# A fused vision block: squeeze gate in fewer steps, projection from the lower half first, the sums x + xn on VectorE, and a new written order

## The chip, the cores and the metric

The kernel runs on one core of a Trainium2 chip. Time is the device time of one launch in microseconds (us); three runs gave 5884.94 to 5890.72, median 5888.1. The engines are TensorE (PE, its weight loads PEld), VectorE (DVE), ScalarE (ACT), GpSimd (POOL) and SyncE (SP), which issues all DMAs here. Each works through its own list of instructions in order, and they wait for each other by semaphores.

## The reference

The input is 32 images of 96 channels, 56 x 56. Two layers follow, each a convolution part and a feed-forward part with its own norm and residual. The part that the change touches is layer 0's convolution:

```python
h = einsum('nchw,oc->nohw', x, w_exp)            # 96 -> 576
h = silu(bn(h));  h = silu(bn(depthwise3x3(h)))
s = h.mean(axis=(2, 3))
s = silu(s @ w_se1.T + b_se1)                    # 576 -> 24
s = sigmoid(s @ w_se2.T + b_se2)                 # 24 -> 576
h = einsum('nchw,oc->nohw', h * s, w_proj)       # 576 -> 96
return bn(h) + identity                          # identity is the normed x
```

The image is normed before (xn), and x + xn is what the projection is added to. Behind it come a quantised feed-forward part (96 to 384 to 96, in 8-bit floats), layer 1's convolution (1x1, group norm, gelu, axial shifts by one pixel with 1x1 convolutions and gelus, group norm, 1x1) and a second feed-forward part.

## The kernel before

An image is 96 channels of 3136 positions, cut into eight tiles of seven rows (392 positions); tiles 0 to 3 are the upper half, 4 to 7 the lower. The work is software-pipelined over images: one frame of the program holds layer 0's convolution of image i, and parts of images i+1 (its first norm and expansions), i-1 and i-2. What each engine does in a frame and in which order is written out by hand: the table `TIMES` (lines 52 to 134) gives each step a number per engine, and `timetable` sorts by them. The numbers set the order only. `with_banks` deals three PSUM banks (the ring) to the steps in that order.

The steps that are named here, a step being what one tile or one chunk needs on one engine:
- center_a, var_a, rstd_a, norm_a: the first norm of image i+1. GpSimd's norm_a (line 1110) adds xn to x in the buffer x_in; save_s stores the sum to DRAM, reload_x loads x a second time ahead of it, fetch_s brings the sum back for the projection.
- expand k, dw k h: the 576 channels are five chunks (four and a half). Chunks 0 to 2 are expanded on TensorE and convolved on VectorE, nine taps for each half h of the image (line 965; the first tap, line 962, opens the accumulator). Half 0 of chunk 0 and the rest go through texp and tconv, a convolution on TensorE.
- silu2: ScalarE's activation of the convolved maps, with the channel sums for the gate.
- se1, se2, se3: the gate. TensorE multiplies 21 columns of sums by w_se1 (line 660), ScalarE takes the silu, TensorE multiplies by w_se2 (line 666), VectorE adds the bias (969), ScalarE takes tanh, VectorE makes 0.5 t + 0.5 (972) and scales the projection's weights (977, 979).
- proj: six steps (line 671 and on), three for the upper half and then three for the lower. Each makes one tile whole and a third of the half's fourth tile. x1 (lines 988, 992) adds the projection to x + xn.
- center 0, var 0, rstd 0, norm 0, up, down, add: norm and feed-forward part; the same with 1 and 2 for the later norms.
- conv1, gn, gelu1, shift, combo, fold, sum, conv3, x2: layer 1's convolution. The group norm's chain (lines 1045 to 1077) runs over VectorE, TensorE and GpSimd (the root).

The tap that opens an accumulator of chunk 0 or 1 waits until all six projections of the image before are done, since the projection reads the same buffers.

## Time and profile before

| | before |
|---|---|
| median of 3 runs | 5888.1 us (5884.94 to 5890.72) |
| the profiled execution | 5895.56 us, of which the span of its instructions is 5893.7 us |
| TensorE busy | 5303.1 us, 90% of the span |
| VectorE busy | 4892.0 us, 83% |
| ScalarE busy | 4145.5 us, 70% |
| GpSimd busy | 574.4 us, 10% |
| mean granted TensorE clock | 0.945 of 2.4 GHz |

Busy time is the time in which an engine has at least one instruction under way. Matmuls overlap, so a full TensorE isn't one at its peak. "Idle before" and "waited for" name what released an engine after it had stood still.

### The profile page before, as it was taken

What the parts mean: (1) busy time and instruction counts of PE and PEld (TensorE: products, weight loads), DVE (VectorE), ACT (ScalarE), POOL (GpSimd) and SP (SyncE); (2) the same over time, 40 slices, a digit from 0 to 9 for tenths busy, and PEclk for the clock granted to TensorE, in tenths of its full rate; (3) what the DMA queues carried; (4) which work ended last, traced back from release to release, by engine and by line L of the source; (5) the groups of instructions that cost most, each with busy time, mean ns of one, the idle gap of its engine ahead of it and who ended that gap; (6) DMA issues with size and microseconds to landing.
All of it is one profiled execution on the core that took longest, in us unless ns stands there. A gap on an engine that the chain in (4) does not pass through costs nothing.

```text
span 5893.7 us, 165528 instructions
## 1 busy us (share of the span) xinstructions
PE 5303.1 (90%) x67266; PEld 2773.9 (47%) x67266; DVE 4892.0 (83%) x8119; ACT 4145.5 (70%) x7517; POOL 574.4 (10%) x431
## 2 busy tenths in 40 slices
PE   1889999999999999999999999999999998999986
PEld 0344555444555444555444555444555444555442
DVE  4878988888988888988888988888988888988874
ACT  1467766677867677777767867767867777867766
POOL 1111001111001111001111001111001111001100
PEclk9999999999999999999999999999999999999997
DMA  1334434444433444443444434445443445443433
GB/s 51 84 100 122 105 99 103 116 116 125 105 100 101 115 115 122 105 102 102 117 115 126 102 101 104 118 111 126 102 102 102 116 114 125 104 101 100 113 79 78
DMA packets 467883, 625.04 MB, mean 106 GB/s; under 512 B 81218, under 2 KB 466691, under 8 KB 467035
## 3 DMA queue, kind: packets, MB, share of 16 engines
q1 hardware_dynamic: 467132, 614.44, 41.2%
q8 instruction: 543, 8.90, 0.7%
q14 instruction: 208, 1.70, 0.1%
HBM read 272.13 MB, written 78.68 MB: 60 GB/s over the span
## 4 chain that ended last, share of the span: by engine, by line
PE 51%; issue 24%; DVE 8%; ACT 6%; POOL 6%; DMA 3%; SPq 1%; POOLq 0%; ACTq 0%; DVEq 0%
PE bank L596 21%; PE bank L650 11%; PE b_banks L596 7%; POOL x_in L1110 6%; PE bank L637 4%; PE sums_b L603 3%; PE sums_a L603 2%; DVE conv L965 2%; DMA x_in<-in_x 2%; ACT hidden L879 2%; PE bank L679 1%; ACT hidden L886 1%; DVE bn_stats L1037 1%; PE bank L666 1%; PE bank L660 1%
## 5 line engine op out<-in xcount | busy, mean ns | idle before, releaser
L965 DVE SCALAR_TENSOR_TENSOR conv<-mid,w_dw,conv 128x1568 f32<-128x1568 f32 x1280 | 2339.8, 1843 | 3.6
L761 PE MATMUL b_banks<-shifted,w_combo 128*32 128x392 f32 x6144 | 639.8, 543 | 179.8 <-DMA shifted<-g 115.7
L596 PE MATMUL bank<-xc_a,w_exp 128*32 128x392 f32 x5376 | 714.8, 509 | 43.7 <-DVE xc_a L948 38.7
L1110 POOL TENSOR_TENSOR x_in<-x_in,xc_a 96x392 f32<-96x392 f32 x256 | 509.7, 2000 | 1731.4 <-DVE xc_a L948 1125.4
L679 PE MATMUL bank<-conv,w_proj_gated 128*32 128x392 f32 x1920 | 665.7, 503 | 0.0
L596 PE MATMUL bank<-conv,w_proj_gated 128*32 128x392 f32 x5760 | 652.7, 495 | 0.2 <-DVE w_proj_gated L979 0.2
L596 PE MATMUL bank<-x,centering 128*32 128x392 f32 x4608 | 646.3, 504 | 1.5 <-ACT sq_a L790 0.5
L650 PE MATMUL bank<-phases,w_toeplitz 128*32 128x392 f32 x6144 | 645.1, 494 | 0.8 <-ACT phases L823 0.7
L879 ACT ACTIVATE hidden<-b_banks 128x1176 f16<-128x1176 f32 x512 | 590.6, 1153 | 40.5 <-PE b_banks L596 36.9
L637 PE MATMUL bank<-xc_a,w_exp 128*32 128x448 f32 x4096 | 593.6, 545 | 15.8 <-ACT mid L816 15.4
L886 ACT ACTIVATE hidden<-hidden 128x1176 fp8e5<-128x1176 f16 x512 | 607.3, 1186 | 0.8 <-PE bank L596 0.7
L650 PE MATMUL bank<-phases_on,w_toeplitz 128*32 128x392 f32 x6144 | 598.6, 494 | 2.6 <-DMA phases_on<-phases 2.6
L596 PE MATMUL b_banks<-xn,w_q 128*32 128x392 fp8e5 x6144 | 519.1, 344 | 78.8 <-DVE xn L1014 41.1
L789 ACT ACTIVATE xc<-bank 96x392 f32<-96x392 f32 x256 | 126.3, 493 | 549.6 <-PE sums_a L603 443.5
L834 ACT ACTIVATE conv<-bank,bn_affine 128x392 f32<-128x392 f32 x512 | 347.1, 678 | 192.4 <-PE bank L650 191.6
L988 DVE SCALAR_TENSOR_TENSOR x<-bank,bn_bias,r_a 96x392 f32<-96x392 f32 x192 | 119.4, 622 | 426.9 <-PE bank L679 318.7
L761 PEld LDWEIGHTS b_banks<-shifted,w_combo 128*32 128x32 f32 x6144 | 217.4, 116 | 540.7 <-DMA shifted<-g 276.6
L603 PE MATMUL sums_a<-sq_a,row_select 128*32 128x98 f32 x4096 | 448.5, 256 | 1.5 <-ACT sq_a L790 1.5
L816 ACT ACTIVATE mid<-bank 128x392 f32<-128x392 f32 x672 | 336.5, 501 | 140.1 <-PE bank L596 132.8
L603 PE MATMUL sums_b<-sq_b,row_select 128*32 128x98 f32 x4096 | 421.0, 248 | 1.7 <-ACT sq_b L870 0.8
L1022 DVE TENSOR_SCALAR hidden<-hidden,b_q 128x392 f16<-128x392 f16 x1536 | 397.1, 312 | 18.4 <-ACT hidden L879 17.1
L596 PEld LDWEIGHTS bank<-conv,w_proj_gated 128*32 128x32 f32 x5760 | 230.1, 111 | 379.9 <-issue 370.3
(165 smaller groups left out, 9279.0 us busy)
## 6 DMA issues: line engine op xcount, KB each, us to landing
phases_on<-phases SPq DMA_DIRECT2D x1024, 101.5 KB, 2.4
shifted<-g SPq DMA_DIRECT2D x512, 149.6 KB, 2.7
x_in<-in_x SPq DMA_DIRECT2D x512, 147.0 KB, 2.7
shifted<-g SPq DMA_DIRECT2D x256, 199.5 KB, 3.0
r_a<-rstd_row_a SPq DMA_DIRECT2D x256, 147.0 KB, 3.2
x_plus_norm<-x_in SPq DMA_DIRECT2D x256, 147.0 KB, 2.6
r_b<-rstd_row_c SPq DMA_DIRECT2D x256, 147.0 KB, 2.9
r_b<-rstd_row_b SPq DMA_DIRECT2D x256, 147.0 KB, 2.8
```

The source lines that it names most:

```text
L596: last = mm(o[j:j + QUAD, :], weights[:, j:j + QUAD], x, start=start, stop=stop)
L603: last = mm(VPS[th], ROW[:, VR - 1 - r:VR - 1 - r + QUAD], sq[:, j * VW:(j + 1) * VW], start=(r == 0), stop=(r == VR - 1))
L637: last = mm(ring[bank][32 * q:32 * q + 32, 0:EROWS * WW], WEXP[:, m0:m0 + 32], xc_phase(q, h), start=True, stop=True)
L650: last = mm(ring[bank][32 * p:32 * p + 32, 0:TW], TWZ[:, (3 * g + dx) * 2 + r % 2, :], phase_rows(EB if r < 2 else FB, p, QH, dx), start=( ...
L679: last = mm(ring[bank][C:C + QUAD, 0:TW], weights[:, QUAD * r:QUAD * r + QUAD], tile(maps, NTH - 1, 128), start=start, stop=stop)
L761: last = mm(rows(PB[32 * u:32 * u + 32, m, 0:TW]), WC[:, u // 2, 32 * m:32 * m + 32], SH[t % 2][:, u, :].rearrange("p (h w) -> p h w", w=G ...
L834: f(conv_rows(u, r), rows(ring[bank][:, 0:TW]), ACT.Silu, scale=SCB[:, 0, k:k + 1], bias=SCB[:, 1, k:k + 1], accum_out=SUMS[:, j:j + 1]).t ...
L879: f(Y16[t % 2][:, :, :], PB[:, 0:NHC, 0:TW], ACT.Copy).then_inc(sem["up_evacuated"], 1)
L886: f(Q8[t % 2][:, :, :], Y16[t % 2][:, :, :], ACT.Copy, saturate=False)\
L965: v.scalar_tensor_tensor(out=acc, in0=src, scalar=WDW[:, k, j:j + 1], in1=acc, op0=ALU.mult, op1=ALU.add).then_inc(convolved, 1)
L1022: last = v.tensor_scalar(Y16[t % 2][:, c, :], Y16[t % 2][:, c, :], B1Q[:, g, c:c + 1], 0.0, ALU.add, ALU.max)
L1110: g.tensor_tensor(xl, xl, xc_tile(t), ALU.add).then_inc(sem["xplus_a"], 1)
```

## The change

Five things are changed.

1. The gate. The matmuls over the channel sums are split: 20 of the 21 columns (step se1a) stand ahead, and one, the last half of chunk 2, is left for se1. They write into the bank of the sums of squares, not into the ring. The bias of the second product is a row of its weights (S1 has a constant one below its 24 rows), and this product is made in groups of 32 columns. Tanh reads PSUM, and the 0.5 of 0.5 t + 0.5 is folded into the projection's weights at setup, so that the gated weights are WP t + WP, one VectorE instruction for each of six slices.
2. The projection. The lower half comes first, and a projection waits for each slice of the gated weights by itself, not for all. Everything that follows the order of its tiles (x1, center 0, var 0, the last feed-forward part, store) is turned by four tiles (`turned`).
3. The tap that opens the lower half of chunk 0 or 1 waits for the first three projections of the image before, and the upper half's for all six.
4. The sums x + xn are a VectorE step, xplus_a; GpSimd has none left.
5. `TIMES` has new numbers throughout, so every engine's order is another one.

```diff
     "DVE": {
-        "rstd_a": (5168,), "norm_a": (5622, 5814, 5991, 6773, 6831, 7212, 7671, 7960),
-        "dw 0 1": (8759, 9328, 9453, 9691, 9806, 9869, 9928, 9984, 10404),
+        "xplus_a": (6291, 6995, 7187, 7884, 7974, 8001, 8773, 9160), "rstd_a": (5187,),
+        "dw 0 1": (8468, 8491, 8661, 8691, 8998, 9338, 9348, 9402, 9427),
...
+    def turned(t):
+        return (t + NTH) % NT
...
+            elif name in ("se1a", "se1"):
                 chunk_of = [0] + [k for k in range(1, NDV) for _ in range(2)] + [0] * PH + [NDV] * (2 * PH) + [NCH] * PH
+                late = N_S2 - 1
+                if name == "se1a":
+                    pe.wait_ge(sem["activated2"], at(N_S2 * a + late))
+                    pe.wait_ge(sem["t_activated2"], at(N_TC * (a + 1)))
+                    pe.wait_ge(sem["se_scalar"], at(2 * a - 1))
+                    for j, k in enumerate(chunk_of):
+                        if j != late:
+                            mm(SE1P, SE1[:, k, :], SUMS[:, j:j + 1], start=(j == 0), stop=False)
+                else:
+                    pe.wait_ge(sem["activated2"], at(N_S2 * (a + 1)))
+                    mm(SE1P, SE1[:, chunk_of[late], :], SUMS[:, late:late + 1], start=False, stop=True)
...
                 for k in range(NCK):
-                    last = mm(ring[bank][:, k:k + 1], SE2[:, 128 * k:128 * k + 128], S1, start=True, stop=True)
+                    last = columns(ring[bank][:, k:k + 1], SE2[:, 128 * k:128 * k + 128], S1)
...
                 for k in range(NCH + 1):
-                    weights = WPS[:, k if k < NCH else NCH + h, :]
-                    maps = conv(k, h) if k < NCH else ACC4
+                    if r == 0 and (h == 0 or k == NCH):
+                        pe.wait_ge(sem["se_vector"], at((NCK + 1) * a + (k + 1 if h == 0 else NCK + 1)))
+                    weights = WPS[:, k if k < NCH else NCH + 1 - h, :]
+                    maps = conv(k, 1 - h) if k < NCH else ACC4
...
+            elif name == "se2":
+                act.wait_ge(sem["se_matmul"], at(2 * a + 2))
+                act.wait_ge(sem["se_vector"], at((NCK + 1) * a))
+                f(GATE[:, :], ring[bank][:, 0:NCK], ACT.Tanh, scale=0.5).then_inc(sem["se_scalar"], 1)
...
+            elif name == "xplus_a":
+                t = arg[0]
+                dve.wait_ge(sem["normed_a"], at(NT * n + t + 1))
+                dve.wait_ge(x_loaded[t % XSLOTS], at(16 * (NT // XSLOTS * (2 * n + 1) + t // XSLOTS + 1)))
+                xl = XL[t % XSLOTS][0:C, :]
+                v.tensor_tensor(xl, xl, xc_tile(t), ALU.add).then_inc(sem["xplus_a"], 1)
...
                     if k <= 1:
-                        dve.wait_ge(sem["projected"], at(NPR * m))
+                        dve.wait_ge(sem["projected"], at(NPR * (m - 1) + NTH - 1 if h else NPR * m))
...
-                v.tensor_tensor(WPS[:, 0:NCK, :], WP[:, 0:NCK, :],
-                                GATE[:, 2, :].unsqueeze(2).to_broadcast([128, NCK, C]), ALU.mult)
-                v.tensor_scalar(WPS[CW:128, NCK, :], WP[CW:128, NCK, :], GATE[CW:128, 2, NCH:NCK], None, ALU.mult)\
-                    .then_inc(sem["se_vector"], 1)
+                for k in (*range(NCH), NCK, NCH):
+                    p0, p1, g = (CW, 128, NCH) if k == NCK else (0, CW, k) if k == NCH else (0, 128, k)
+                    v.scalar_tensor_tensor(out=WPS[p0:p1, k, :], in0=WP[p0:p1, k, :], scalar=GATE[p0:p1, g:g + 1],
+                                           in1=WP[p0:p1, k, :], op0=ALU.mult, op1=ALU.add).then_inc(sem["se_vector"], 1)
...
-            elif name == "norm_a":
-                t = arg[0]
-                pool.wait_ge(sem["normed_a"], at(NT * n + t + 1))
```

VectorE, from the gated weights to the middle of the projection, before. L969 to L979 is the gate, L1029 and L1032 an add of the feed-forward part, L988 and L992 are one x1, L1087 is x2, L962 the first tap of the lower half of chunk 0:

```order
L969 TENSOR_TENSOR gate<-bank,b_se 128x5
L972 TENSOR_SCALAR gate<-gate 128x5
L977 TENSOR_TENSOR w_proj_gated<-w_proj,gate 128x480
L979 TENSOR_SCALAR w_proj_gated<-w_proj,gate 64x96
...
L1087 SCALAR_TENSOR_TENSOR x<-b_banks,gn_small,x 96x392
...
L992 SCALAR_TENSOR_TENSOR x<-bank,bn_bias,xc 32x392
L962 TENSOR_SCALAR conv_1<-mid,w_dw 128x1568
L988 SCALAR_TENSOR_TENSOR x<-bank,bn_bias,r_a 96x392
L992 SCALAR_TENSOR_TENSOR x<-bank,bn_bias,xc 32x392
L965 SCALAR_TENSOR_TENSOR conv_1<-mid,w_dw,conv_1 128x1568
```

The same place on VectorE after (L967 is x + xn, L991 a slice of the gated weights, L1000 and L1004 x1, L1100 x2, L980 and L983 taps):

```order
L967 TENSOR_TENSOR x_in<-x_in,xc_a 96x392
L991 SCALAR_TENSOR_TENSOR w_proj_gated<-w_proj,gate 128x96 x4
L991 SCALAR_TENSOR_TENSOR w_proj_gated<-w_proj,gate 64x96 x2
L967 TENSOR_TENSOR x_in<-x_in,xc_a 96x392 x2
...
L1004 SCALAR_TENSOR_TENSOR x<-bank,bn_bias,xc 32x392
L1100 SCALAR_TENSOR_TENSOR x<-b_banks,gn_small,x 96x392
L980 TENSOR_SCALAR conv_1<-mid,w_dw 128x1568
L983 SCALAR_TENSOR_TENSOR conv_1<-mid,w_dw,conv_1 128x1568
L1100 SCALAR_TENSOR_TENSOR x<-b_banks,gn_small,x 96x392
L983 SCALAR_TENSOR_TENSOR conv_1<-mid,w_dw,conv_1 128x1568 x2
L967 TENSOR_TENSOR x_in<-x_in,xc_a 96x392
L1000 SCALAR_TENSOR_TENSOR x<-bank,bn_bias,r_a 96x392
```

Before, the lower half's first tap stood ahead of the last x1 (fifth x1 above it, sixth below) and the others behind it; now it and three more stand between the third and the fourth x1. The sums of x stand ahead of the gated weights and behind them.

TensorE, from the second group norm's last product (L747) to the first projection, before (L660 is se1, L666 se2, b_banks from g conv3, bank from xc_a an expansion, centering a center):

```order
L747 MATMUL sums_b<-gn_small,w_l 96x1
L660 MATMUL bank<-pool_sums,w_se 24x1 x21
L596 MATMUL b_banks<-g,w_scaled 32x392 x6
L666 MATMUL bank<-x 128x1 x5
L596 MATMUL b_banks<-g,w_scaled 32x392 x3
L596 MATMUL bank<-xc_a,w_exp 32x392 x4
L596 MATMUL bank<-x,centering 32x392 x3
L596 MATMUL bank<-conv_0,w_proj_gated 32x392 x3
```

And after (L667 is se1a, L670 se1, bank from x with 32x1 se2):

```order
L667 MATMUL sums_a<-pool_sums,w_se 24x1 x20
L599 MATMUL bank<-xc_a,w_exp 32x392 x4
L758 MATMUL sums_b<-gn_small,w_l 96x1
L670 MATMUL sums_a<-pool_sums,w_se 24x1
L599 MATMUL bank<-xc_a,w_exp 32x392 x4
L599 MATMUL bank<-x 32x1 x20
L599 MATMUL b_banks<-g,w_scaled 32x392 x3
L599 MATMUL bank<-xc_a,w_exp 32x392 x4
L599 MATMUL bank<-conv_1,w_proj_gated 32x392 x3
```

Twenty of the gate's products moved ahead of the group norm's, and two of three conv3 and the center moved behind the start of the projection.

TensorE between the third projection and the fourth, after; before, nothing stood there:

```order
L599 MATMUL bank<-x,centering 32x392 x3
L599 MATMUL b_banks<-g,w_scaled 32x392 x3
L599 MATMUL bank<-x,centering 32x392 x6
L607 MATMUL sums_a<-sq_a,row_select 32x98 x4
L599 MATMUL b_banks<-g,w_scaled 32x392 x3
L599 MATMUL bank<-x,centering 32x392 x3
L599 MATMUL bank<-conv_0,w_proj_gated 32x392 x3
```

Six three-column steps now stand in the middle of the projection.

## Rows read from the trace of the kernel before

**Rows 1.** The page: busy time of each engine, its share of the span, instructions.
```profile
PE 5303.1 (90%) x67266; PEld 2773.9 (47%) x67266; DVE 4892.0 (83%) x8119; ACT 4145.5 (70%) x7517; POOL 574.4 (10%) x431
```
**Rows 2.** Busy time in one frame: engine, busy (instructions); PEclk, DMA share, GB/s.
```profile
2700.00:2874.20 174.20, 162.74 (x2098) 85.35 (x2094) 149.63 (x247) 129.21 (x235) 17.68 (x13) 0.96 0.43 108
```
**Rows 3.** The same in slices: PE, PEld, DVE, ACT, POOL; PEclk, DMA, GB/s.
```profile
2866.00:2876.00 10.00, 8.29 (x99) 4.28 (x102) 6.92 (x16) 2.74 (x9) 2.45 (x3) 0.83 0.58 162
2886.00:2896.00 10.00, 10.00 (x130) 4.35 (x125) 3.76 (x6) 0.00 (x0) 1.02 (x1) 1.00 0.35 96
2916.00:2926.00 10.00, 10.00 (x144) 5.79 (x138) 10.00 (x14) 7.92 (x15) 0.00 (x0) 1.00 0.32 80
```
**Rows 4.** TensorE's waits over the span: for whom; us, times, longest.
```profile
PE b_banks L761 <- DMA shifted<-g: 115.7, 89, 7.1
...
PE sums_b L747 <- DVE gn_small L1070: 55.0, 32, 2.5
...
PE bank L596 <- DVE w_proj_gated L979: 0.2, 1, 0.2
```
**Rows 5.** VectorE's timeline: start, duration, instruction [idle before, releaser].
```profile
2810.39 0.36 DVE L1045 BATCH_NORM_AGGREGATE gn_small<-bn_stats 96x2 f32<-96x48 f32 x1
...
2831.16 0.27 DVE L933 TENSOR_SCALAR r_a<-sums_a 32x98 f32<-32x98 f32 x1 [3.06 <-issue]
...
2861.32 0.37 DVE L1045 BATCH_NORM_AGGREGATE gn_small<-bn_stats 96x2 f32<-96x48 f32 x1
...
2865.52 0.97 DVE L1066 TENSOR_TENSOR gn_small<-gn_small,v_l 96x1 f32<-96x1 f32 x1 [0.44 <-POOL gn_small L1104]
2866.53 0.93 DVE L1068 TENSOR_TENSOR gn_small<-gn_small 96x1 f32<-96x1 f32 x1
...
2873.60 0.15 DVE L969 TENSOR_TENSOR gate<-bank,b_se 128x5 f32<-128x5 f32 x1
...
2896.64 1.04 DVE L962 TENSOR_SCALAR conv<-mid,w_dw 128x1568 f32<-128x1568 f32 x1 [2.00 <-PE bank L679]
```
**Rows 6.** TensorE's timeline, with the same columns (x: instructions merged into the row).
```profile
2794.46 1.17 PE L596 MATMUL b_banks<-g,w_l 128*32 128x392 f32 x9
...
2810.80 0.33 PE L740 MATMUL sums_b<-gn_small,mean_w 96*96 96x1 f32 x2 [0.24 <-DVE gn_small L1045]
...
2821.64 4.15 PE L761 MATMUL b_banks<-shifted,w_combo 128*32 128x392 f32 x24 [1.46 <-DMA shifted<-g]
...
2833.26 2.18 PE L761 MATMUL b_banks<-shifted,w_combo 128*32 128x392 f32 x24
...
2871.97 1.27 PE L666 MATMUL bank<-x 24*128 24x1 f32 x10
...
2875.22 0.52 PE L596 MATMUL bank<-conv,w_proj_gated 128*32 128x392 f32 x2
...
2896.31 1.17 PE L596 MATMUL bank<-x,centering 128*32 128x392 f32 x9
```
**Rows 7.** VectorE's groups by form: count | busy us, mean ns | idle before.
```profile
L965 DVE SCALAR_TENSOR_TENSOR conv<-mid,w_dw,conv 128x1568 f32<-128x1568 f32 x1280 | 2339.8, 1843 | 3.6
...
L948 DVE TENSOR_TENSOR xc_a<-xc_a,r_a 96x392 f32<-96x392 f32 x256 | 154.7, 604 | 23.0 <-DMA r_a<-rstd_row_a 22.8
...
L1070 DVE TENSOR_TENSOR gn_small<-v_l,gn_small 96x1 f32<-96x1 f32 x64 | 9.9, 155 | 2.2
...
L979 DVE TENSOR_SCALAR w_proj_gated<-w_proj,gate 64x96 f32<-64x96 f32 x32 | 8.6, 270 | 0.5
```
**Rows 8.** GpSimd's waits, then its group of sums.
```profile
POOL x_in L1110 <- DMA x_in<-in_x: 606.0, 96, 10.7
...
L1110 POOL TENSOR_TENSOR x_in<-x_in,xc_a 96x392 f32<-96x392 f32 x256 | 509.7, 2000 | 1731.4 <-DVE xc_a L948 1125.4 <-DMA x_in<-in_x 606.0
```
**Rows 9.** ScalarE's timeline: the last silu ahead of the gate, and its Tanh.
```profile
2864.57 1.70 ACT L845 ACTIVATE conv<-conv,bn_affine 128x1568 f32<-128x1568 f32 x1
...
2873.78 0.21 ACT L854 ACTIVATE gate<-gate 128x5 f32<-128x5 f32 x1 [3.02 <-DVE gate L969]
```

132 lines of the change are left out of this document (58 added, 74 removed), and 102 rows, old and new, of the table TIMES.

## Prediction

> **What bounds the kernel now.** I read the page's busy line first, then one frame (one image's turn of the pipeline, 174.2 us here), then ten-microsecond slices of it. TensorE is busy for 5303 of 5894 us, VectorE for 4892 [rows 1]. In the frame TensorE is busy for 162.7 us, VectorE for 149.6 [rows 2], so TensorE idles for 11.5 us and VectorE for 24.6, and the question is where. The slices answer it: in the projection VectorE works 3.76 of 10 us while TensorE is full; just behind it both are full; around the gate TensorE is short, with the granted clock at 0.83 [rows 3]. VectorE can't start the next depthwise taps in the projection: tap 0 of "dw 0 1" is released by the last projection tile at 2896.64 [rows 5]. TensorE's waits lie elsewhere, in the grouped convolution between the two group norms: for the shifted copies 115.7 us in total, for the second norm's affine 55.0. For the gated weights it waited 0.2 us [rows 4].
>
> TensorE's landmarks cut the frame into stages [rows 6]; the projection's start is 2875.22 and its end the 2896.64 of [rows 5]:
> - conv1 (2794.46) to gn 0 (2810.80): 16.3 us, full.
> - gn 0 to gn 1, by VectorE's aggregates 2810.39 and 2861.32 [rows 5]: 50.9 us. TensorE has gaps, VectorE one of 3.06 us, in which rstd_a waits for the sums of squares.
> - aggregate of gn 1 to projection: 13.9 us.
> - projection: 21.4 us.
> - projection's end to the next conv1 (2794.46 + 174.2 = 2968.7): 72.0 us, TensorE full.
> These are 174.5 us for 174.2, since two boundaries are read on another engine.
>
> **The change, part by part.** A three-column step on TensorE (center, conv1, conv3) is two groups of x3; nine instructions took 1.17 us, the last 0.51, so a group costs 0.33 and a step 0.66 [rows 6]. An expansion of four columns has two groups too.
>
> *Gate chain.* Before, from the gate's first VectorE instruction (2873.60) to the first projection matmul it was 1.6 us [rows 5, 6]: an addition, Tanh on ScalarE, an affine, the product over all chunks, and the split chunk's 0.27. Center and expansions covered it, hence the wait of 0.2 us. After, Tanh reads PSUM and VectorE writes six slices of 96 columns; the nearest row is 0.27 us for 64x96 [rows 7], and TensorE may start after the first. Six cost up to 1.6 us of VectorE; the old instructions took the 1.6 us less 0.2 of Tanh [rows 9]: equal. The chain is 1 us shorter and TensorE's second gate step turns from 5 matmuls of 128 columns into 20 of 32; I take that step as unchanged (it took 1.27 us for ten instructions [rows 6]; between half and one and a half times that, so ±0.65). What pays is the order. From the aggregate of gn 1, VectorE has two moved sums and norms, the spread and the last tap of "dw 2 1", about 3.6 us; ScalarE's silu of that half is 1.7 us [rows 9] and its sum is read out behind it, so 5.5; one matmul is left of the first gate step, since the 20 others (1.3 us) went ahead; then two short ScalarE steps [rows 9] around the second gate step, 1.3: 8.2 us to the first slice (5.5 + 0.3 + 0.4 + 1.3 + 0.4 + 0.3), 8.9 when the conv3 and the expansion behind that step are counted. TensorE's own work in the stage falls by 2.0 less 0.7: two conv3 and one center moved behind the start of the projection, an expansion came in. The stage was 13.9; I take 10.4, **-3.5 us**, for what in-order queues will add, with ends 9.4 (-4.5) and 12.9 (-1.0). Two VectorE instructions of the affine took 0.97 and 0.93 us beside GpSimd's sums, where a like one takes 0.155 [rows 5, 7]. That 1.6 us of stretch is part of the gain.
>
> *Projection.* Between proj.0 and proj.5 TensorE now has seven three-column steps instead of two, and two of var: 5 x 0.66 + 0.2 = **+3.5 us**. VectorE gets four more taps, two more x2, one add and one sum there; four taps are 7.4 us at 1.843 [rows 7]. With the others it is some 10 us, and the stage has room: VectorE idled for 6.2 of 10 us in it [rows 3], 13 of the 21.4. Taps on the lower half don't touch the accumulator tiles that the remaining matmuls read. The lower half goes first because the waiting accumulator is the lower one. A late reload of x + xn for x1.3 is now covered by the four taps ahead of it.
>
> *Behind the projection.* Two centers fewer and one expansion of phases fewer up to conv1: -2.1; var pairs -0.1: **-2.2 us**, and the expansion comes back in the next stage, **+0.6**. That 7 us of taps are gone here is worth nothing: TensorE is full [rows 3].
>
> *Group norm 0 to 1.* Taps (17), adds, quants and norms of x are equal in number before and after. One fp8 norm and one sum x + xn are added, 2 x 0.604 = +1.2 [rows 7]; two adds and a norm, 2.2 us of work, moved ahead of rstd_a and fill as much of the gap of 3.06 [rows 5]: -2.2 + 1.2 = **-1.0**. Ends: -1.9, the whole gap filled, and 0, where ScalarE or the shifted copies hold the stage.
>
> *Sums x + xn on VectorE.* Eight of 0.604 are 4.8 us a frame on an engine of 149.6 [rows 2, 7]; GpSimd took 2.0 us each [rows 8]. Of the eight, one is counted above, four lie in the gate stage and three in the projection and behind it. Only what stands ahead of the gate slices counts, and it is in the 8.2 us.
> What the rows show of the shared work is that VectorE's small instructions stretch from 0.155 to 0.97 beside a GpSimd sum [rows 5, 7], while a GpSimd sum stretches to a mean of 2.0 [rows 8]. The Trainium skill ("SBUF — State Buffer", Who interferes with whom) has a rule for that: a VectorE instruction with two SBUF inputs and a GpSimd instruction that reads SBUF exclude each other; the trace agrees.
> VectorE is the second busiest engine, and 1.2 us of new work stand in its fullest stage [rows 1, 2]. The Trainium skill ("Perfetto Trace Analysis", Optimizing Scalar/DVE Operations) would rather move work from a saturated VectorE to GpSimd, but adds that the shared port may void that; by it this change goes the wrong way, which is rival 3.
>
> **The sum.** -3.5 + 3.5 - 2.2 + 0.6 - 1.0 = -2.6 us a frame. With 32 images there are 31 frames from gate to gate: -81 us. Setup gains two short VectorE instructions, under 1 us. The profiled execution took 5895.6 us (span 5893.7); 5895.6 - 81 = 5814.6. The runs' median, 5888.1, is 7.5 lower: **5807 us**. Ends: -4.5 - 1.9 - 2.2 + 0.6 + 3.5 = -4.5 a frame, 5749 us; -1.0 + 0 - 2.2 + 0.6 + 3.5 = +0.9, 5916.
>
> **Rivals.**
> 1. *More comes back.* The first combo took 4.15 us for 24 matmuls that take 2.18 later; ahead of it TensorE had gapped and was at the half clock [rows 6]. If the gaps close, the clock stays up: -2.0 more than the best sum, -6.5 x 31 = -202: 5687 us. For it: both low-clock places lie behind gaps. Against: that combo's gap is a chain (norm, gelu, five copies) that the change hardly touches.
> 2. *Nothing.* VectorE was not what held the combo stage; the copies were (115.7 us) [rows 4], and ScalarE has no less to do. Then group norm 0 to 1 gives 0, the gate stage gives what was moved out of it, 2.0, and its smaller gap 1.6, the projection takes 3.5: -3.6 + 3.5 - 2.2 + 0.6 = -1.7 less what the second gate step costs more, 0.65, and a like amount lost at banks: about -0.4 x 31: 5876 us. For it: TensorE is full in three stages, 16.3 + 21.4 + 72.0 us, and its work is unchanged.
> 3. *The in-order queue pays for GpSimd's waits.* GpSimd waited 606 us for the reload of x, 96 times, 6.3 us each [rows 8], and nobody stood behind it. On VectorE one such sum stands directly ahead of the gate slices and two more ahead of x1.0. The projection's first tile (a sixth of 21.4 - 1.3, 3.3 us) hides two; the one ahead of the slices hides nothing. If the reload lands late there, the gate and the projection start 6.3 us late: -2.6 + 6.3 = +3.7 a frame, 6003 us. It decides from 2.6 us of lateness on. Against: for that sum, tile 3, the reload waits for no store of a slot but only for the centering of all eight tiles, which is done before the combos; tiles 4 and on wait for a store.
> 4. *The stage is VectorE's.* The adds and the order fill it, with its slack in the projection spent, and it ends 1 us later than the middle: -1.0 in the gate stage and +1.2 between the norms: +2.1 a frame: 5953 us.
>
> **How the numbers follow.** Forecast (5749 to 5860) 0.46; rival 1 0.18; rival 2 (5860 to 5900) 0.16; rivals 3 and 4 0.20, of which half lies under 5940. What can be told from no change is 0.2%, 12 us: 5876 to 5900. Faster: 0.46 + 0.18 + 0.07 = 0.71, same 0.11, slower 0.18. The range runs from rival 1 to 5930: 0.08 left out below, 0.1 above.
>
> **What would show it.** Right: the 24 us of VectorE's idleness per frame shrink, with five taps between x1.0 and x1.5; the idle time ahead of rstd_a's first instruction is under 1 us; the aggregate of gn 1 to the first projection matmul is near 10 us; the affine's multiplications take 0.16 us; busy TensorE time is the same. Wrong: VectorE waiting for x_in at its sums; TensorE waiting for w_proj_gated by more than 1 us a frame; TensorE waiting longer for the shifted copies; x1.3 or a center between the projections waiting for a bank. If the gate stage is short and the frame isn't, the loss lies where TensorE was full.

## The result, and the profile after

The changed kernel takes 5681.5 us (median of 4 runs, 5676.0 to 5687.2) where the kernel before took 5889.4 in the same comparison: a ratio of 0.9643, interval 0.9625 to 0.9662. That is 208 us, 3.5%, less. In a second comparison it was 0.9630 (0.9613 to 0.9648). The forecast was 5807 us with a range of 5685 to 5930: the direction was right, the gain was two and a half times the forecast one, and the time lies 3.5 us below the range.

The page of the changed kernel, busy line, answers to [rows 1]:

```profile
PE 5167.6 (91%) x68226; PEld 2777.0 (49%) x68226; DVE 4964.0 (87%) x8441; ACT 4168.4 (73%) x7517; POOL 77.3 (1%) x175
```

TensorE is busy for 135.5 us less, although it has 960 matmul records more. A busy time that shrinks under more work points at the clock: the mean granted clock went from 0.945 to 0.970, up 2.6%, and the busy time fell by 2.6%. VectorE is busy for 72 us more and GpSimd for 497 less.

How long a frame is in the mean, from the first and the last time of the gate's first VectorE instruction. Before, then after (L991 has six instructions a frame, and the row's last start is that of the last one, 1.4 us after its first):

```profile
L969 DVE TENSOR_TENSOR gate<-bank,b_se x32: 148/165/166, 234.8 to 5695.7; 128x5 f32<-128x5 f32 x32
```
```profile
L991 DVE SCALAR_TENSOR_TENSOR w_proj_gated<-w_proj,gate x192: 308/315/321, 234.9 to 5480.9; 128x96 f32<-128x96 f32 x128, 64x96 f32<-64x96 f32 x64
```

(5695.7 - 234.8) / 31 is 176.2 us, and (5480.9 - 1.4 - 234.9) / 31 is 169.2. So a frame lost 7.0 us, and the frame of 174.2 us on which the prediction stood [rows 2] was 2 us shorter than the mean.

The stages of that other, commoner kind of frame before. The columns are those of [rows 2]: stretch, its length, busy time (instructions) of PE, PEld, DVE, ACT, POOL, granted clock, DMA share, GB/s. Second group norm to projection, projection, projection to the next conv1:

```profile
2683.93:2699.51 15.58, 13.10 (x121) 6.54 (x122) 11.15 (x24) 6.12 (x11) 3.76 (x4) 0.73 0.56 155
2699.51:2722.26 22.75, 22.75 (x272) 9.51 (x269) 6.89 (x12) 3.13 (x7) 2.04 (x2) 0.96 0.35 105
2722.26:2794.46 72.20, 71.79 (x1055) 45.47 (x1051) 70.52 (x122) 60.88 (x114) 0.00 (x0) 1.00 0.26 67
```

The frame that the prediction used, first two of these stages:

```profile
2861.32:2875.22 13.90, 11.52 (x126) 5.15 (x122) 10.28 (x23) 6.62 (x13) 3.77 (x4) 0.88 0.55 151
2875.22:2896.49 21.27, 21.27 (x266) 9.28 (x266) 7.75 (x13) 2.73 (x7) 2.05 (x2) 1.00 0.44 127
```

The matmuls and the order are the same in both frames. In the first one the granted clock is 0.73 and 0.96, in the second 0.88 and 1.00, and the two stages together take 38.3 us against 35.2. "Half clock" below is the time in which the granted clock was 1.2 GHz instead of 2.4. The record of the granted clock gives it for these two stages: 10.2 us in 20 of the 30 whole frames before, 6.8 in 2, 3.4 in 7, none in one.

All five stages of a frame after, of the kind without any half clock in the gate (conv1, group norm 0, group norm 1, projection, projection's end to the next conv1):

```profile
1850.20:1865.98 15.78, 15.78 (x193) 8.22 (x191) 15.60 (x24) 12.87 (x30) 0.31 (x3) 1.00 0.39 111
1865.98:1915.79 49.81, 40.64 (x477) 18.46 (x472) 47.19 (x74) 44.88 (x74) 1.27 (x1) 0.93 0.68 166
1915.79:1924.43 8.64, 8.00 (x150) 3.96 (x145) 7.50 (x22) 8.11 (x15) 0.55 (x1) 1.00 0.69 194
1924.43:1949.52 25.09, 25.09 (x313) 13.37 (x307) 19.65 (x28) 4.79 (x11) 0.00 (x0) 1.00 0.39 119
1949.52:2019.36 69.84, 69.84 (x1026) 43.30 (x1020) 62.28 (x117) 59.45 (x109) 0.00 (x0) 1.00 0.27 66
```

After, 19 of the 30 frames have no half clock in the gate and the projection, and 11 have 3.4 us. Means over the 30 frames from conv1 to conv1, in us (from the same landmarks as in [rows 5, 6]):

| stage, mean us | before | after | difference | forecast |
|---|---|---|---|---|
| conv1 to group norm 0 | 16.04 | 15.98 | -0.1 | +0.6 |
| group norm 0 to 1 | 50.90 | 49.46 | -1.4 | -1.0 |
| group norm 1 to projection | 15.07 | 8.97 | -6.1 | -3.5 |
| projection | 22.24 | 25.24 | +3.0 | +3.5 |
| projection to next conv1 | 72.20 | 69.87 | -2.3 | -2.2 |
| frame | 176.45 | 169.53 | -6.9 | -2.6 |
| half clock, gate and projection | 8.07 | 1.25 | -6.8 | |
| half clock, group norm 0 to 1 | 9.44 | 5.92 | -3.5 | |

Where the half clock began, before. TensorE's timeline in the commoner frame (start, duration, instruction, idle before it and its releaser):

```profile
2690.32 0.33 PE L747 MATMUL sums_b<-gn_small,w_l 96*96 96x1 f32 x2 [1.70 <-DVE gn_small L1070]
...
2692.55 2.18 PE L596 MATMUL b_banks<-g,w_scaled 128*32 128x392 f32 x9
...
2694.66 2.29 PE L666 MATMUL bank<-x 24*128 24x1 f32 x10
```

Behind the gap of 1.70 us and the small gate products, nine matmul records of conv3 take 2.18 us, where nine took 1.17 at the full clock, and the second gate step takes 2.29 where it took 1.27 [rows 6]. The gap itself was 1.70 us in each of the 30 frames, in the one without half clock too. The same place after, in a frame without half clock, with its largest gap:

```profile
1921.62 0.33 PE L758 MATMUL sums_b<-gn_small,w_l 96*96 96x1 f32 x2
1922.27 0.21 PE L670 MATMUL sums_a<-pool_sums,w_se 128*24 128x1 f32 x2 [0.32 <-ACT conv L856]
1922.37 0.87 PE L599 MATMUL bank<-xc_a,w_exp 128*32 128x392 f32 x8
1923.17 0.50 PE L599 MATMUL bank<-x 32*32 32x1 f32 x40
```

And VectorE's affine in a later frame, which [rows 5] had at 0.97 and 0.93 us, with the end of the gate:

```profile
2770.47 0.15 DVE L1079 TENSOR_TENSOR gn_small<-gn_small,v_l 96x1 f32<-96x1 f32 x1
2770.66 0.15 DVE L1081 TENSOR_TENSOR gn_small<-gn_small 96x1 f32<-96x1 f32 x1
...
2774.18 1.70 DVE L991 SCALAR_TENSOR_TENSOR w_proj_gated<-w_proj,gate 128x96 f32<-128x96 f32 x6 [1.50 <-ACT gate L866]
```

TensorE's waits after, to be read against [rows 4]: the copies as before, the affine 2.3 us instead of 55.0. The last line is VectorE's wait for the reload of x:

```profile
PE b_banks L772 <- DMA shifted<-g: 117.4, 109, 2.7
...
PE sums_b L758 <- DVE gn_small L1083: 2.3, 3, 1.5
...
DVE x_in L967 <- DMA x_in<-in_x: 2.5, 1, 2.5
```

### The profile page after: what moved, and what is told of

The parts are those of the page before. It is cut to its first block, busy times and chain, and to the rows that moved or that the text cites. A ratio compares the mean times of both kernels' runs of the same rounds, so it can differ in the third digit from the quotient of the medians.

```text
span 5680.9 us, 167481 instructions
## 1 busy us (share of the span) xinstructions
PE 5167.6 (91%) x68226; PEld 2777.0 (49%) x68226; DVE 4964.0 (87%) x8441; ACT 4168.4 (73%) x7517; POOL 77.3 (1%) x175
## 4 chain that ended last, share of the span: by engine, by line
PE 62%; DVE 12%; ACT 9%; SPq 8%; DMA 5%; issue 4%; POOL 1%; ACTq 0%; DVEq 0%
PE bank L599 25%; PE bank L654 12%; PE b_banks L599 7%; DVE conv L983 4%; PE bank L641 4%; PE sums_b L607 4%; PE b_banks L772 4%; PE bank L689 3%; SPq L553 3%; SPq L557 2%; DMA shifted<-g 2%; PE sums_a L607 2%; ACT conv L856 2%; DMA r_b<-rstd_row_b 1%; ACT hidden L898 1%
## 5 line engine op out<-in xcount | busy, mean ns | idle before, releaser
L983 DVE SCALAR_TENSOR_TENSOR conv<-mid,w_dw,conv 128x1568 f32<-128x1568 f32 x1280 | 2341.3, 1844 | 12.5
L599 PE MATMUL bank<-xc_a,w_exp 128*32 128x392 f32 x5376 | 753.4, 503 | 29.7 <-DVE xc_a L960 29.4
L772 PE MATMUL b_banks<-shifted,w_combo 128*32 128x392 f32 x6144 | 593.7, 514 | 180.9 <-DMA shifted<-g 117.4
L689 PE MATMUL bank<-conv,w_proj_gated 128*32 128x392 f32 x1920 | 653.5, 495 | 0.0
L599 PE MATMUL bank<-conv,w_proj_gated 128*32 128x392 f32 x5760 | 651.6, 493 | 0.0
L654 PE MATMUL bank<-phases,w_toeplitz 128*32 128x392 f32 x6144 | 631.9, 492 | 0.7 <-ACT phases L834 0.7
L599 PE MATMUL bank<-x,centering 128*32 128x392 f32 x4608 | 627.9, 495 | 0.9 <-ACT sq_a L801 0.5
L599 PE MATMUL b_banks<-xn,w_q 128*32 128x392 fp8e5 x6144 | 503.0, 346 | 92.3 <-ACT hidden L891 79.9
L641 PE MATMUL bank<-xc_a,w_exp 128*32 128x448 f32 x4096 | 572.8, 546 | 10.8 <-ACT mid L827 7.9
L599 PEld LDWEIGHTS bank<-conv,w_proj_gated 128*32 128x32 f32 x5760 | 261.2, 110 | 296.2 <-issue 212.8
L599 PE MATMUL bank<-hidden,w_q 128*32 128x392 fp8e5 x4608 | 367.9, 345 | 41.0 <-ACT sq_a L801 34.1
L607 PEld LDWEIGHTS sums_b<-sq_b,row_select 128*32 128x32 f32 x4096 | 352.5, 110 | 65.8 <-issue 39.8
```

What stands on the lines that cost most here:

```text
L599: last = mm(o[j:j + QUAD, :], weights[:, j:j + QUAD], x, start=start, stop=stop)
L607: last = mm(VPS[th], ROW[:, VR - 1 - q:VR - 1 - q + QUAD], sq[:, j * VW:(j + 1) * VW], start=(r == 0), stop=(r == VR - 1))
L641: last = mm(ring[bank][32 * q:32 * q + 32, 0:EROWS * WW], WEXP[:, m0:m0 + 32], xc_phase(q, h), start=True, stop=True)
L654: last = mm(ring[bank][32 * p:32 * p + 32, 0:TW], TWZ[:, (3 * g + dx) * 2 + r % 2, :], phase_rows(EB if r < 2 else FB, p, QH, dx), start=( ...
L689: last = mm(ring[bank][C:C + QUAD, 0:TW], weights[:, QUAD * r:QUAD * r + QUAD], tile(maps, NTH - 1, 128), start=start, stop=stop)
L772: last = mm(rows(PB[32 * u:32 * u + 32, m, 0:TW]), WC[:, u // 2, 32 * m:32 * m + 32], SH[t % 2][:, u, :].rearrange("p (h w) -> p h w", w=G ...
```

## The experiments

The labels that begin with b_ are the kernel before with one edit, those with a_ the changed kernel with one edit. The theory after the result was: about half of the gain is TensorE's clock in the gate and the projection, and what keeps it up is that the gaps there are closed. The rival was that the gain is that of the chain and the order, and the clock a bystander. Stage times below are means over 30 frames.

**1. Filling the gap of the kernel before**

```diff
             elif name == "gn_weights":
+                for r in range(5):
+                    columns(PB[0:C, r % 3, 0:TW], CEN[:, :], WEXP[:, 0:TW])
                 pe.wait_ge(sem["gn_affine"], at(GN_P * (2 * b + 2)))
```

> The kernel before with 15 matmuls more per frame (five groups of three, 392 columns of constants, into banks that conv3 overwrites later), put ahead of the last small product of the second group norm, where TensorE stands still for 1.7 us. They compute nothing that is used. Theory A (the clock: TensorE's gap there is what takes the granted clock to half for 10.2 us in two of three frames, and that is about half of what the change won): the gap is gone, the half-clock time at the gate falls from a mean of 8.1 us a frame to under 4, and the frame gets 1.5 to 3 us shorter, 5795 to 5845 us. Theory B (the change won by its order and the shorter chain, the clock follows something else): 1.65 us of idle time is filled and nothing else happens, 5880 to 5900 us; if the filler is late for the product behind it, up to 5940 us.

Measured: 5819.1 us, ratio 0.9875 (0.9858 to 0.9891). More work for TensorE, and 74 us less. TensorE at the fillers, then the stage up to the projection:

```profile
2653.99 3.47 PE L596 MATMUL b_banks<-w_exp,centering 128*32 128x392 f32 x30
2657.39 0.33 PE L749 MATMUL sums_b<-gn_small,w_l 96*96 96x1 f32 x2
```
```profile
2649.31:2663.05 13.74, 13.53 (x164) 5.92 (x156) 10.01 (x23) 6.72 (x13) 3.78 (x4) 1.00 0.56 155
```

No frame has half clock there any more, and every one takes 35.1 us for the two stages (mean before: 37.3). That is theory A, inside its range. But the expectation had the filler's size wrong: each of these matmuls has two records (x30 for 15), a group of three takes 0.66 us, and five are 3.47 us in a gap of 1.70. The product behind them comes late. (The same error of two stands in the sizes that the expectations of b_dve_fill, b_dve_fill2 and a_fill_gate give.) With two groups:

> b_fill5 with two groups instead of five. A group of three matmuls is 0.66 us in the trace, not 0.33 as was taken for the runs so far (each of these matmuls has two records), so five were 3.3 us in a gap of 1.70; two are 1.32 us. In b_fill5 the stage up to the projection was 13.7 us without any half clock; the one undisturbed frame of the kernel before took 12.0. If the excess of the fillers was on the path and two groups still keep the clock up: 1.6 us a frame less than b_fill5, 5760 to 5780 us, and gate and projection at 33.5 us in nearly all frames. If two groups leave gap enough for the clock to fall in some frames: 5785 to 5840 us.

Measured: 5777.7 us, ratio 0.9802 (0.9784 to 0.9820). The two stages:

```profile
2630.45:2643.33 12.88, 11.50 (x138) 5.25 (x134) 10.76 (x23) 7.14 (x14) 3.80 (x4) 1.00 0.62 178
2643.33:2664.60 21.27, 21.27 (x263) 9.26 (x266) 7.75 (x13) 2.34 (x6) 2.04 (x2) 1.00 0.41 117
```

No half clock in any of the 30 frames, and the two stages take 33.8 us in the mean. That is the clock alone, with order, chain and sums as in the kernel before: 3.5 us a frame for 8.07 us of half clock, and 2% of the kernel. The rival, that the clock is a bystander, falls.

**2. The sums on VectorE alone**

```diff
     "DVE": {
-        "rstd_a": (5168,), "norm_a": (5622, 5814, 5991, 6773, 6831, 7212, 7671, 7960),
+        "xplus_a": (6065, 7211, 7486, 7929, 8107, 8300, 8674, 9100), "rstd_a": (5168,), "norm_a": (5622, 5814, 5991, 6773, 6831, 7212, 7671, 7960),
...
     "POOL": {
-        "norm_a": (2245, 2298, 3298, 4019, 4530, 5386, 5455, 10126), "gn 0": (20768,), "root 0": (21305,),
+        "gn 0": (20768,), "root 0": (21305,),
...
```

With it, the step's code moves from GpSimd's list to VectorE's (`xplus_a`, as in the changed kernel).

> The kernel before with the sums x + xn as VectorE steps (at places in its order that answer to those of the changed kernel) and nothing else. Theory A with GpSimd's sums as the cause of the gap: the two multiplications of the second affine take 0.16 us instead of 0.97 and 0.93, TensorE's gap ahead of that product falls from 1.7 to under 0.5 us, the half clock at the gate gets rarer, 5740 to 5850 us. Theory B (part 4 is not what pays): the sums cost 4.8 us of VectorE a frame in an order that has no room for them, 5889 to 5990 us.

Measured: 5797.8 us, ratio 0.9839 (0.9820 to 0.9857), 95 us less. Part 4, which rival 3 and rival 4 held to be the dangerous one, pays by itself. VectorE's affine and TensorE's remaining gap, in the frame behind 2650:

```profile
2655.81 0.15 DVE L1072 TENSOR_TENSOR gn_small<-gn_small,v_l 96x1 f32<-96x1 f32 x1 [0.44 <-POOL gn_small L1110]
2656.00 0.15 DVE L1074 TENSOR_TENSOR gn_small<-gn_small 96x1 f32<-96x1 f32 x1
```
```profile
2655.42 0.86 PE L596 MATMUL bank<-xc_a,w_exp 128*32 128x392 f32 x8 [0.90 <-DVE xc_a L948]
2656.40 0.33 PE L747 MATMUL sums_b<-gn_small,w_l 96*96 96x1 f32 x2
```

The gap of 1.70 us is gone, one of 0.90 is left a little earlier. The stage up to the projection is 12.63 us instead of 15.07, and the frames fall into kinds by their half clock: 13 frames without it take 32.8 us for the two stages, 8 frames with 3.4 us of it 34.4, 6 with 6.8 us 36.1, 3 with 10.2 us 37.8. So 3.4 us of half clock cost about 1.65 us, half of its length. Against frames of the kernel before with as much half clock the two stages are 0.7 us shorter (32.8 to 33.5 without any, 34.4 to 35.1 with 3.4 us); the rest of what this edit gains there is the clock.

**3. The sums on GpSimd in the changed kernel**

```diff
     "DVE": {
-        "xplus_a": (6291, 6995, 7187, 7884, 7974, 8001, 8773, 9160), "rstd_a": (5187,),
+        "rstd_a": (5187,),
...
     "POOL": {
-        "gn 0": (22416,), "root 0": (22893,), "root 1": (23987,),
+        "xplus_a": (3000, 3100, 3200, 4019, 4530, 5386, 5455, 12126), "gn 0": (22416,), "root 0": (22893,), "root 1": (23987,),
...
```

> The changed kernel with the sums x + xn back on GpSimd, in GpSimd's old order. If the sums' contention is what holds the affine and with it the clock: the affine's multiplications are back near 0.95 us, the stage from the aggregate of the second group norm to the projection is 2 to 4 us longer, 5740 to 5820 us. If not: VectorE loses 4.8 us of work a frame, and the time is 5640 to 5695 us.

Measured: 5766.0 us, ratio 0.9783 (0.9761 to 0.9805); the changed kernel has 0.9643, so 84 us more. The affine's group and the wait for it:

```profile
L1073 DVE TENSOR_TENSOR gn_small<-gn_small,v_l 96x1 f32<-96x1 f32 x64 | 34.7, 542 | 15.0 <-POOL gn_small L1117 15.0
```
```profile
PE sums_b L758 <- DVE gn_small L1077: 43.2, 32, 1.5
```

The mean of 542 ns is that of two group norms a frame, one at 0.15 us and one near 0.95, as before the change. The half clock in gate and projection is back to 4.8 us a frame. Edits 2 and 3 agree from both sides: 95 and 84 us.

**4. The changed code in the old order**

TIMES is that of the kernel before, with the new steps where their work stood:

```diff
-        "tconv 2": (13017, 13271, 13321, 13350), "tconv 3": (14170, 14640, 15995, 16279), "se1a": (17184,),
...
+        "tconv 2": (13113, 13178, 13291, 13314), "tconv 3": (13760, 14148, 15660, 16150), "se1a": (17381,), "se1": (17382,),
...
-        "dw 0 1": (8468, 8491, 8661, 8691, 8998, 9338, 9348, 9402, 9427),
...
+        "dw 0 1": (8759, 9328, 9453, 9691, 9806, 9869, 9928, 9984, 10404),
```

> The changed kernel's code (split gate chain, slices, lower half first, sums on VectorE, early release of the lower half) in the written order of the kernel before; the new steps stand where their work stood. If the order is what pays (the theory that the gain is the shorter chain made visible by moving an expansion ahead and conv3 and centers behind): 5800 to 5900 us. If the parts pay without the order: 5690 to 5770 us.

Measured: 5730.9 us, ratio 0.9724 (0.9704 to 0.9744): 162 of the 208 us without the new order. A frame:

```profile
2612.28:2622.72 10.44, 9.13 (x158) 3.82 (x153) 9.21 (x25) 6.55 (x12) 0.80 (x1) 1.00 0.55 143
2622.72:2644.60 21.88, 21.88 (x273) 9.57 (x269) 9.48 (x19) 3.13 (x7) 0.00 (x0) 1.00 0.51 147
2644.60:2717.66 73.06, 72.45 (x1055) 45.48 (x1050) 71.53 (x124) 61.10 (x114) 0.00 (x0) 1.00 0.27 68
```

Gate and projection take 32.7 us in the mean, with 0.9 us of half clock, which is 1.5 us less than in the changed kernel; what lies behind takes 72.3 instead of 69.9. So the first four changes keep the clock up here without the new order, and the taps of "dw 0 1" stand behind the projection, as in the kernel before. The order moves work into the projection; over the frame it is worth 1.3 us (170.8 to 169.5).

**5. The two parts of the gate, each undone in the changed kernel**

```diff
-        "tconv 2": (13017, 13271, 13321, 13350), "tconv 3": (14170, 14640, 15995, 16279), "se1a": (17184,),
+        "tconv 2": (13017, 13271, 13321, 13350), "tconv 3": (14170, 14640, 15995, 16279), "se1a": (17292,),
```

> The changed kernel with the 20 early products of the gate standing directly ahead of the last one, behind the expansion and the last product of the group norm, as before the change. They took 1.14 us of TensorE for 40 instructions. If the split is worth its own work on the path (1.1 us a frame) and a wider gap brings back some half clock: +1.1 to +2.5 us a frame, 5715 to 5760 us. If the other work hides it (the last silu ends later anyway): 5675 to 5695 us.

```diff
-                    if r == 0 and (h == 0 or k == NCH):
-                        pe.wait_ge(sem["se_vector"], at((NCK + 1) * a + (k + 1 if h == 0 else NCK + 1)))
+                    if r == 0 and h == 0 and k == 0:
+                        pe.wait_ge(sem["se_vector"], at((NCK + 1) * (a + 1)))
```

> The changed kernel with its first projection waiting for all six slices of the gated weights at once. If the slices' early start is on the path: the projection begins up to 1.4 us later, with the gap's half clock up to 2 us a frame: 5725 to 5745 us. If conv3 and the expansion that stand ahead of the projection cover it, as the wait of 0.2 us in the kernel before would have it: 5675 to 5690 us.

Measured: without the split 5726.6 us, ratio 0.9713 (0.9696 to 0.9730), 45 us more than the changed kernel; without the wait by slices 5709.3 us, 0.9681 (0.9661 to 0.9702), 28 us more. Both are on the path; the second time lies between the two ranges of its expectation. Without the split the gate stage is 0.8 us longer and the half clock 2.7 us a frame instead of 1.25. The single wait costs 1.26 us in the gate stage, near the 1.4 us from the first to the last slice, and 0.6 us of it comes back in the projection; the half clock is 1.6 us a frame, so these 28 us are not the wait alone. "Conv3 and the expansion cover it" was wrong.

**6. The taps back behind the projection**

```diff
-        "dw 0 1": (8468, 8491, 8661, 8691, 8998, 9338, 9348, 9402, 9427),
+        "dw 0 1": (9051, 9052, 9053, 9054, 9055, 9338, 9348, 9402, 9427),
```

> The changed kernel with the four taps of dw 0 1 and its first one, which stand in the projection, moved behind the last x1 and the work in the same place (9 us of VectorE are idle in the projection again). The prediction's claim is that they are worth nothing there, since TensorE is full behind the projection: 5675 to 5700 us. The rival: VectorE is full behind the projection, falls behind there and holds the group norm: +3 to +7 us a frame, 5770 to 5900 us.

Measured: 5897.8 us, ratio 1.0003 (0.9991 to 1.0015). The whole gain is gone. Gate and projection are those of the changed kernel (8.9 and 25.2 us), but what lies behind takes 76.8 us instead of 69.9. VectorE there, then TensorE, then TensorE's wait over the whole span:

```profile
2716.53 7.51 DVE L983 SCALAR_TENSOR_TENSOR conv<-mid,w_dw,conv 128x1568 f32<-128x1568 f32 x4
2724.07 0.62 DVE L1100 SCALAR_TENSOR_TENSOR x<-b_banks,gn_small,x 96x392 f32<-96x392 f32 x1
```
```profile
2724.75 0.88 PE L599 MATMUL b_banks<-g,w_scaled 128*32 128x392 f32 x3 [4.07 <-DVE x L1100]
```
```profile
PE b_banks L599 <- DVE x L1100: 121.9, 30, 4.1
```

A conv3 waits for its bank, which x2 has to read, and x2 stands behind four taps. The gap of 4.07 us brings 5.0 us of half clock with it. Is it only where x2 stands? The same taps behind x2.3 and x2.4:

```diff
-        "dw 0 1": (8468, 8491, 8661, 8691, 8998, 9338, 9348, 9402, 9427),
+        "dw 0 1": (9296, 9297, 9298, 9299, 9300, 9338, 9348, 9402, 9427),
```

> The changed kernel with the same five taps moved out of the projection as in a_taps_late, but behind x2.3, x2.4 and the sum of tile 7, so that conv3 does not wait for its banks behind them. If the 7 us that a_taps_late lost were only the order (x2 behind the taps): 5680 to 5720 us. If the sum of VectorE's work behind the projection binds (7.4 us of taps for 6.64 us of idle time there): at least 1 us a frame more and the half clock behind the projection again, 5720 to 5900 us.

Measured: 5940.9 us, ratio 1.0088 (1.0072 to 1.0105), worse still, and above both ranges. TensorE now waits for the quantised norm of the next stage:

```profile
PE b_banks L599 <- DVE xn L1026: 206.4, 33, 7.9
```

The stage behind the projection, with the taps behind the last x1 and then behind x2.3 and x2.4:

```profile
2713.99:2791.63 77.64, 73.57 (x1025) 44.03 (x1020) 71.93 (x122) 59.59 (x109) 0.00 (x0) 0.96 0.25 61
```
```profile
2746.50:2824.97 78.47, 72.24 (x1026) 43.59 (x1020) 72.07 (x122) 60.08 (x109) 0.00 (x0) 0.96 0.23 61
```

The four taps and the opening one are 8.4 us, and the changed kernel's VectorE idles for 6.64 us there in the mean, so the stage would have to grow by some 2 us for the sum of VectorE's work alone. It grew by 7.0 and 8.7 us, and VectorE still idles for 5.7 and 6.4 us in the frames shown. The rest is a wait in its in-order list that TensorE feels (4.07 us in the first frame, 6.23 in the second) and the half clock that follows it (5.0 and 6.8 us a frame). Experiment 4 has nearly as much VectorE work in this stage, 71.53 us, and takes 73.06: with the old order the same taps fit. So what these two runs show is that the new order, which took work off TensorE here, has no place for the taps behind the projection; that no order has one is not shown.

**7. Filling the gaps behind the first group norm, in the changed kernel**

```diff
             elif name == "up":
                 f, t = arg
+                if f == 1 and t == 6:
+                    pe.wait_ge(sem["gn_vector"], at(GN_V * (2 * min(b, NIMG - 1) + 1)))
+                    for r in range(8):
+                        columns(small_b[0:C, 128:384], CEN[:, :], WEXP[:, 0:256])
...
             elif name == "down":
                 f, t = arg
+                if f == 1 and t == 4:
+                    pe.wait_ge(sem["gn_vector"], at(GN_V * (2 * min(b, NIMG - 1) + 1)))
+                    for r in range(5):
+                        columns(small_b[0:C, 128:384], CEN[:, :], WEXP[:, 0:256])
```

> The changed kernel with 39 matmuls more per frame (256 columns of constants into unused columns of a PSUM bank, in groups of three), eight groups ahead of up 1.6 and five ahead of down 1.4, where TensorE stands still for 2.04 and 1.43 us behind the first group norm. They compute nothing that is used. If these gaps are what takes the clock to half at the first combos (5.9 us a frame) and the first combos are on the path: -0.5 to -1.6 us a frame, 5630 to 5665 us. If the stage is held by VectorE and the copies, a faster combo waits longer for its copy: 5670 to 5690 us. Against both: fillers that delay up 1.6 would give 5690 to 5710 us.

Measured: 5705.6 us, ratio 0.9675 (0.9658 to 0.9692), 24 us more. The half clock between the norms fell from 5.9 to 1.0 us a frame, and the stage grew from 49.46 to 50.06 us. The run does not settle it: its first filler was 3.4 us in a gap of 2.04, and its second stood behind the first combo. With fillers that fit (four groups, and two ahead of down 1.3 instead of down 1.4):

> The changed kernel with four filler groups of 256 columns (some 1.7 us) in the gap of 2.04 us ahead of up 1.6 and two (0.85 us) in the gap of 1.43 us ahead of down 1.3. a_fill_combo had twice as much, which delayed up 1.6 by over a microsecond, and its second filler stood behind the first combo. If the half clock at the first combos (5.9 us a frame) costs something that the oversized fillers hid: 5645 to 5670 us. If the stage is held by VectorE and the copies whatever the clock: 5672 to 5684 us.

Measured: 5663.1 us (5645.5 to 5665.4), ratio 0.9600 (0.9579 to 0.9621). A frame's stretch between the norms, with the fillers and in the changed kernel:

```profile
2536.73:2585.25 48.52, 41.50 (x513) 18.99 (x509) 47.15 (x74) 45.06 (x74) 1.27 (x1) 1.00 0.70 171
```
```profile
2545.19:2594.68 49.49, 40.72 (x477) 18.53 (x472) 47.09 (x74) 44.86 (x74) 1.27 (x1) 0.93 0.69 168
```

In the mean the stage takes 49.21 us, with 1.5 us of half clock; the changed kernel has 49.46 with 5.9, and in its second profile 49.26 with 5.1. So 3.6 to 4.4 us less half clock bring between 0.05 and 0.25 us a frame in this stage, 2 to 8 us in all, where 8 us at the gate brought 3.5 a frame. VectorE is busy for 47 of the 49 us here, and a faster first combo meets it and the copies. The total does not quite agree: 5663.1 lies in the range that the expectation gave for a half clock that costs something, 12 to 18 us under the changed kernel's two medians, which come from other comparisons. The stages say that this half clock is nearly free; the time leaves room for a little more.

**8. Sums on VectorE and filled gap together, in the kernel before**

The five groups of experiment 1 in the kernel of experiment 2:

> The kernel before with the sums on VectorE (as b_dve_sums) and the five filler groups of b_fill5. b_dve_sums still had 3.3 us of half clock a frame at the gate, b_fill5 none; a microsecond of half clock cost 0.27 us there (2.2 us less for 8.07 us less). If clock and gap are the two ways in which the sums' place acts, the fillers take away the rest of the half clock and give 0.9 us a frame less what the fillers delay (their 1.65 us now meet a gap of 0.9): 5760 to 5810 us. If the filler's gain in b_fill5 was something else and adds in full: 5710 to 5735 us.

Measured: 5837.4 us, ratio 0.9918 (0.9900 to 0.9937): 40 us more than the sums alone. Neither theory's number. TensorE's timeline tells why:

```profile
2669.00 0.87 PE L596 MATMUL bank<-xc_a,w_exp 128*32 128x392 f32 x8 [0.91 <-DVE xc_a L950]
2669.68 3.47 PE L596 MATMUL b_banks<-w_exp,centering 128*32 128x392 f32 x30
2673.08 0.33 PE L749 MATMUL sums_b<-gn_small,w_l 96*96 96x1 f32 x2
```
```profile
2673.45 0.15 DVE L1085 TENSOR_TENSOR gn_small<-sums_b,v_l 96x1 f32<-96x1 f32 x1 [3.22 <-PE sums_b L749]
```

The fillers stand behind the remaining gap, not in it, and all their 3.47 us are on the chain: VectorE waits 3.22 us for the product behind them. The clock was up (0.1 us of half clock), the frame was longer. So the run told what a filler on the chain costs, not what the gap does. The same kernel with two groups (1.3 us) at the gap itself:

```diff
             elif name == "expand":
                 k, t = arg
+                if k == 0 and t == 3:
+                    for r in range(2):
+                        columns(PB[0:C, r, 0:TW], CEN[:, :], WEXP[:, 0:TW])
```

> The kernel before with the sums on VectorE (as b_dve_sums) and two filler groups of three matmuls (0.66 us) inside the gap of 0.9 us that b_dve_sums still has, ahead of the expansion that waits for the norm. In b_dve_sums the frames without half clock at the gate took 32.8 us from the second group norm to the projection's end, those with 3.4 us of it 34.4. If the gap sets the clock there: nearly all frames are of the first kind, 1 to 1.6 us a frame less, 5750 to 5775 us. If the gap isn't what sets it: 5790 to 5810 us, with as much half clock (3.3 us a frame).

Measured: 5747.2 us, ratio 0.9753 (0.9735 to 0.9770), 51 us less than the sums alone. A frame, gate and projection:

```profile
2616.55:2627.92 11.37, 11.09 (x143) 5.40 (x138) 9.76 (x26) 6.81 (x13) 0.80 (x1) 1.00 0.61 171
2627.92:2649.39 21.47, 21.47 (x269) 10.21 (x266) 9.24 (x16) 2.95 (x7) 0.00 (x0) 1.00 0.46 134
```

29 of 30 frames are of the kind without half clock, at 32.84 us. The gap sets the clock there, with GpSimd's sums gone, and where the filler stands decides.

**9. One filler group in the changed kernel**

```diff
                 else:
+                    columns(PB[0:C, 0, 0:TW], CEN[:, :], WEXP[:, 0:TW])
                     pe.wait_ge(sem["activated2"], at(N_S2 * (a + 1)))
```

> The changed kernel with one filler group of three matmuls (0.33 us) in the gap of 0.32 us ahead of the gate's last first-step product. Ten of its 30 frames still had 3.4 us of half clock there, 1.25 us a frame in the mean. If the gap's closing keeps the clock up: half clock under 0.7 us a frame, -0.1 to -0.4 us a frame, 5668 to 5678 us. If it only delays the product: 5681 to 5692 us.

Measured: 5673.4 us, ratio 0.9634 (0.9618 to 0.9650). Then both in one comparison:

> The changed kernel itself, beside the kernel before and the filled one on the same chip: 5676 to 5687 us, ratio 0.9643.

> The kernel of a_fill_gate again, beside the changed kernel on the same chip. It had no half clock left between the second group norm and the projection's end (1.25 us a frame in the changed kernel). If its 8 us are real: 7 to 12 us under the changed kernel of this comparison. If they were the chip's: within 4 us of it.

Measured: the changed kernel 5675.5 us (5670.8 to 5678.2), with the filler 5662.7 (5657.1 to 5667.2), ratio to the kernel before 0.9611 (0.9594 to 0.9629). It is 12.8 us faster than the changed kernel, and its slowest run is faster than the other's fastest. (The first comparison of the filled kernel gave 5672.4 to 5673.8, as much as the changed kernel here.) Three matmuls that compute nothing take the last half clock out of the gate: none in all 30 frames, where the changed kernel had 3.4 us in 11 frames of its first profile and in 7 of its second:

```profile
1900.56:1909.11 8.55, 8.33 (x153) 4.00 (x149) 7.43 (x22) 7.81 (x15) 0.56 (x1) 1.00 0.65 187
```

They are 0.66 us in a gap of 0.32. Gate and projection together take 33.87 us with them and 33.96 in the changed kernel's second profile, so they win 0.1 us a frame where they stand; another 0.2 lies between the group norms (49.03 against 49.26), and why that stretch got shorter is not shown. Half as many columns (TW // 2), and then that together with the fillers of a_fill_combo2:

> a_fill_gate with matmuls of 196 columns instead of 392: 0.33 us in the gap of 0.32 us, where a_fill_gate put 0.66 us and made the stage 0.25 us longer than the undisturbed frames of the changed kernel. If it keeps the clock up as well: 0.2 us a frame less than a_fill_gate, 5655 to 5668 us. If it is too little for the clock: 5668 to 5682 us.

> a_fill_half and a_fill_combo2 together. If both pay: their gains add, 5620 to 5655 us. If only the gate's filler pays: the time of a_fill_half, within 8 us.

Measured: 5659.8 us (5654.6 to 5667.6), ratio 0.9603 (0.9584 to 0.9621), with the gate stage at 8.54 us instead of 8.77 and no half clock; and 5652.2 us (5645.5 to 5656.2), ratio 0.9587 (0.9569 to 0.9606). The changed kernel was not in this comparison; all runs of both are below its lowest of the others (5670.8). The second is the best version of this study, though its 7.5 us ahead of the first are within what the runs of the two scatter, and it lies in both ranges of its expectation. So a filler in the gate pays some 0.2% of the time, and what that of the combos pays is open.

## Why the prediction fell short, point by point

**What bounds the kernel.** The reading that TensorE is full in three stages and short around the gate stood. The step that failed is the reading of one frame as if it were the mean ("I read ... then one frame"): the frame was one of the 7 of 30 in which only 3.4 us ran at the half clock at the gate. In 22 others it was 6.8 or 10.2 us. The 0.83 of [rows 3] was seen and never priced.

**The missing term.** The sum had no clock term at all: it put at nothing what was worth 3.1 us a frame, more than the whole gain of 2.6 that it forecast. One of its own signs, "busy TensorE time is the same", failed by this: 135.5 us less. Compare frames of equal half clock in the gate and the projection (between the group norms the two kernels still differ, by some 4 us of it, which experiment 7 finds nearly free). With 3.4 us of it, the frame took 174.15 us before (7 frames) and 170.35 after (11 frames): -3.8, of which the stage up to the projection is -4.0 (13.74 to 9.73) and the projection +4.1 (21.39 to 25.52). These two cancel, as they did in the forecast (-3.5 and +3.5). So the -3.1 us by which the two stages together shrank in the mean (37.3 to 34.2) are the half clock, 8.07 us a frame before and 1.25 after. Experiment 1 shows it by moving the clock with the order kept, and the one frame before without half clock agrees: its two stages took 33.5 us, the 19 such frames after 33.6. Experiments 2, 3 and 8 show what moved it, the sums on GpSimd and the gap; 4 shows that the clock stays up (0.9 us of half clock a frame) without the new order. The other 3.8 us are the terms of the sum, forecast as 2.6: conv1 to group norm 0 -0.1 instead of +0.6, since more left the stage than the expansion that came in (193 matmul records in the frame above, 206 in the one at 2794 before); group norm 0 to 1 -1.4 instead of -1.0, with the idle time ahead of rstd_a down from 2.9 us to 0.2 in the mean, as forecast; behind the projection -2.3 instead of -2.2.

**The gate chain.** "What pays is the order" did not hold: experiment 4 has 162 of the 208 us in the old order. "8.2 us to the first slice, 8.9 with conv3 and the expansion" was right: 8.6 us in the frame without half clock. The allowance to 10.4 "for what in-order queues will add" was mis-sized (9.7 us in the frames with as much half clock as the one it was taken from, 8.97 in the mean), and the end of 9.4 was too high as well. The second gate step shrank: 0.50 us at the full clock for its 20 matmuls of 32 columns, where it had taken 1.27. "Center and expansions covered it" was true of the kernel before and false after: experiment 5 prices the split at 45 us and the slices at 28.

**The projection.** +3.0 in the mean and +4.1 at equal clock, forecast +3.5. Its taps did fit: VectorE works 19.65 of its 25.09 us.

**Behind the projection.** The size was right and the reason wrong. "That 7 us of taps are gone here is worth nothing: TensorE is full" looked at one engine. VectorE was just as full there, 70.52 of 72.20 us, so a stage of 69.9 us had no room for its work. Experiment 6 puts them back, and the whole 208 us are gone. But experiment 4 keeps 162 us with the taps behind the projection. So the taps in the projection are no gain by themselves; they are the condition for the new order of the other work, and without them that order costs more than everything else had won.

**Sums x + xn on VectorE.** The prediction counted only the stretch of the affine, 1.6 us, as "part of the gain" and spent more room on the loss. The measured worth is 84 to 95 us, some 3 us a frame: the stretched affine made the gap of 1.70 us, and the half clock over the gate and into the projection fell from 8.07 to 3.30 us a frame when the gap went (experiment 2). Some 0.7 us of the 3 come without the clock.

**The rivals.** Rival 1 has nearly the right number, 5687 us, for the wrong place. It let the clock come back at the first combo; there it is worth 0.25 us a frame at most by the stages of experiment 7, and in the gate it is worth 3.1. Its sum gave 2.0 us to a combo that did get faster (4.1 to 2.7 us in the mean), in a stage that TensorE does not hold. That it names nearly the measured time is luck. Rival 2 was refuted (the stages did shrink). Rival 3 was one wait of 2.5 us in the whole run. Rival 4 was wrong too, though experiment 6 shows how near the new order is to it: 8 us of VectorE's work in the wrong stage are enough.

The Trainium skill ("TensorE: Matmul & The Clock Gate", A second HAM failure mode: psum-queue depth-cycling) tells of another kernel in which frequent short idle times of TensorE between groups of matmuls made the clock go up and down. The gap of 1.70 us ahead of the half clock here agrees. The prediction left it out.

## What to carry to other kernels

Read the granted clock frame by frame, not in one frame, and price it: at the half clock a full TensorE loses nearly half of that time (0.43 to 0.49 us for each microsecond here), and a gap of under 2 us in front of a run of matmuls can be what costs it. Before an engine's work is called free in a stage, ask whether a stage made shorter still has room for every engine's work, in the order in which it is written. And a filler paid here inside a gap of a stage that TensorE holds (up to 3.5 us a frame); behind the gap it cost its own time, and in the stage that VectorE and the copies hold it brought 0.25 us a frame at most by that stage's mean.

## What was not expected of the hardware

- A gap of 0.32 us among small products was followed by 3.4 us of half clock in 11 of 30 frames (7 of 30 in a second profile), and with three short matmuls in it in none.
- The same instructions gave frames of several kinds in one execution: before, 0, 3.4, 6.8 or 10.2 us of half clock in the gate and projection, and frames from 173 to 180 us.
- Work that computes nothing made both kernels faster: 2.0% for the kernel before, 0.2 to 0.5% for the changed one.
- A GpSimd sum of 1 us stretches a VectorE instruction of 0.15 us to 0.95 when both run, and the gap that this makes on TensorE starts a loss several times as long.
- Why one frame gets 3.4 us and the next 10.2 at the same instructions was not settled.
